# Handing tiles to the output stage earlier in a graph message-passing kernel on one Trainium2 core

## The reference

```python
src = node_feature[edge_src]
parts = [relu(node_feature)]
for t in range(3):
    msg = where(edge_type == t, relu(src @ W_e[t].T + b_e[t]), 0)
    parts.append(segment_sum(msg, edge_dst, num_segments=N))
agg = concatenate(parts, axis=1)                       # 6250 x 512
updated[n] = (agg @ W_n[node_type[n]].T + b_n[node_type[n]])[n]
out = layernorm(x + updated + x)
```

## Time and profile before

| | us |
|---|---|
| median of 3 runs | 906.05 (905.99 to 906.22) |
| the profiled execution | 907.5 |
| its span, first to last instruction | 905.7 |
| mean granted PE clock | 0.912 of full speed |

### The profile page before, as it was taken

One profiled execution on the slowest core, in us unless ns is written; L12 is line 12 of the kernel. 1 busy time (PEld: TensorE's weight loads), 2 busy tenths in 40 slices (PEclk: granted clock), 3 DMA queues, 4 the chain that ended last, 5 costly groups with the idle time before them and its releaser, 6 DMA issues.

```text
span 905.7 us, 14050 instructions
## 1 busy us (share of the span) xinstructions
PE 716.2 (79%) x4555; PEld 598.9 (66%) x4555; DVE 616.4 (68%) x1468; ACT 145.0 (16%) x397; POOL 673.7 (74%) x719
## 2 busy tenths in 40 slices
PE   5593056887997988888898878989888798769786
PEld 3362056776876876676687766878767587658674
DVE  7999988476676557557575754775675477656656
ACT  3393000111111101111110120110112011001120
POOL 7777777777777777777777777777777777777772
PEclk9796569998999989999999998999899999989989
DMA  8595533433443343343344342434435334324321
GB/s 245 161 311 147 136 97 76 113 97 50 146 117 105 97 110 107 103 111 92 94 118 116 96 115 78 121 107 111 106 96 114 93 85 118 102 63 128 97 53 45
DMA packets 72065, 101.39 MB, mean 112 GB/s; under 512 B 18137, under 2 KB 55517, under 8 KB 71995
## 3 DMA queue, kind: packets, MB, share of 16 engines
q0 software_dynamic: 22432, 45.99, 21.3%
q1 hardware_dynamic: 46861, 50.45, 18.5%
q10 hardware_dynamic: 2702, 4.08, 1.5%
HBM read 87.47 MB, written 12.97 MB: 111 GB/s over the span
## 4 chain that ended last, share of the span: by engine, by line
POOL 44%; PE 18%; issue 16%; DVE 15%; DMA 6%; SPq 0%; DVEq 0%; POOLq 0%; ACT 0%; ACTq 0%
POOL tab L753 44%; DMA tab<-message_table,idx_t 5%; PE ps L1652 5%; PE ps L1755 3%; PE ps L1673 3%; DVE src_wide L1098 1%; DVE stage L1131 1%; PE ps L1690 1%; PE ps L1686 1%; DVE first_wide L1034 1%; PE ps L1748 1%; DMA dst_raw<-in_dst 1%; PE ps L1631 1%; DVE dst_raw L1091 1%; PE ps L1698 1%
## 5 line engine op out<-in xcount | busy, mean ns | idle before, releaser
L753 POOL DMA_INDIRECT tab<-message_table,idx_t x630 | 595.2, 945 | 194.1 <-issue 185.6
L1652 PE MATMUL ps<-work,tab 128*128 128x126 f32 x1260 | 180.4, 286 | 94.0 <-DMA tab<-message_table,idx_t 68.7
L1252 DVE TENSOR_TENSOR work<-key_t,ps 128x378 f32<-128x378 f32 (+1 forms) x180 | 108.8, 606 | 208.3 <-PE ps L1652 203.7
L1652 PEld LDWEIGHTS ps<-work,tab 128*128 128x128 f32 x1260 | 163.6, 199 | 106.2 <-issue 68.4
L1264 DVE TENSOR_TENSOR acc<-ps,acc 128x126 f32 (+1 forms) x306 | 96.2, 314 | 30.0 <-DVE acc L1264 9.9
L1755 PE MATMUL ps<-wn_t,stage 128*128 128x384 f32 x282 | 104.8, 512 | 0.0
L749 POOL DMA_INDIRECT xg<-in_x,esrc_t x67 | 72.4, 1081 | 20.7 <-issue 16.8
L1755 PEld LDWEIGHTS ps<-wn_t,stage 128*128 128x128 f32 x282 | 56.3, 200 | 40.4 <-issue 5.6
L1673 PE MATMUL ps<-first_wide,tab 128*128 128x128 f32 x450 | 62.8, 291 | 9.5 <-DVE first_wide L1328 6.5
L1673 PEld LDWEIGHTS ps<-first_wide,tab 128*128 128x128 f32 x450 | 58.9, 207 | 9.9 <-issue 9.9
L896 ACT ACTIVATE stage<-ps 128x128 f32<-128x128 f32 x47 | 12.9, 277 | 297.0 <-PE ps L1755 282.1
(11 more groups left out here) (260 smaller groups left out, 1021.4 us busy)
## 6 DMA issues: line engine op xcount, KB each, us to landing
tab<-message_table,idx_t POOLq DMA_INDIRECT x630, 2.6
message_table<-tab SPq DMA_DIRECT2D x24, 384.0 KB, 3.5
dst_raw<-dense_types SPq DMA_DIRECT2D x45, 192.0 KB
wn_raw<-message_table SPq DMA_DIRECT2D x22, 384.0 KB, 3.4
src_wide<-dense_lists SPq DMA_DIRECT2D x45, 128.0 KB, 3.2
we_raw<-early_types SPq DMA_DIRECT2D x18, 192.0 KB
be_b<-early_types SPq DMA_DIRECT2D x18, 192.0 KB
work<-in_x ACTq DMA_DIRECT2D x10, 256.0 KB, 5.0
```

The costliest lines, as they stand in the source:

```text
L753: pool.indirect_dma_start(msg[:, slot, :], None, table, bass.IndirectOffsetOnAxis(ap=rows, axis=0)).then_inc(signal, 16)
L1252: dve.tensor_tensor(hot[:, first:first + n, :].rearrange("p c (t w) -> p c t w", w=WIN), keys.broadcast_to((P, n, T, WIN)), iota_win.rearr ...
L1652: ins = pe.matmul(sums_bank(j, g), msg[:, column, :], hot[:, column, :], start=(c == 0), stop=(c == n - 1))
```

## The change

- `TAKEN_LATE` goes from 3 to 2: 42 tiles are finished in the quarters, and only tiles 42, 43 and 44 in the last iteration.
- `tile_turns` gives each tile its first quarter. Up to tile 32 it is 4(t+3) as before. From tile 33 on it is the latest of 4(t+2), the dense round's quarter `turn_at(t+1)` + 3, and three quarters after the tile before: 143, 146, 150, 153, 156 for tiles 33 to 37, then 160, 164, 168, 172 for 38 to 41. Before, tiles 33 to 37 had 144, 148, 152, 156, 160, and tile 41 came in the last iteration.
- The last extra tile's linear product moves from quarter 154 to 156.
- In PE's quarter `finish_linear` now stands ahead of `place_selfs`. ACT masks a tile's self messages two quarters ahead of its turn.
- In the last iteration PE does both remaining linear products ahead of the last group's sum, and only the three type products of tile 44 after it. Tile 43's accumulator is read once groups 0 and 1 of the last iteration are added. For that the check gets a bound: the last row must not start below node 5632 (`affine_select` on `limit`, with a wait for the iota ahead of it).
- SP stores in another order at the end; `finish_h` gets a wait for the DVE's own `finish_y` of the tile before.

```diff
-TAKEN_LATE, LATE = 3, 4
+TAKEN_LATE, LATE = 2, 4
+def tile_turns():
+    at = []
+    for t in range(SPLIT):
+        if t < LEAD_FROM - LATE + 1:
+            at.append(NG * (t + LATE - 1))
+        else:
+            at.append(max(NG * (t + LATE - 2), turn_at(t + 1) + ADD_LATER - ACC_LATER, at[-1] + NG - 1))
+    return at
...
-LINEAR_AT = [next(q for q in range(at + 2, at + 6) if q % NG == 2) for at in EXTRA_AT]
+LINEAR_AT = [next(q for q in range(at + 2, at + 8)
+                  if (q % NG == 2 or q >= NG * LEAD_FROM) and tile_step(q, LINEAR_LATER) is None
+                  and tile_step(q - 1, LINEAR_LATER) is None) for at in EXTRA_AT]
...
             pool.iota(limit[:, :], pattern=[[P // 2, 2]], base=-P, channel_multiplier=P // 2,
-                      allow_small_or_imprecise_dtypes=True)
+                      allow_small_or_imprecise_dtypes=True).then_inc(limit_made, 1)
+            pool.wait_ge(limit_made, 1)
+            pool.affine_select(out=limit[:, :], in_=limit[:, :], compare_op=ALU.not_equal, fill=float(NA * P),
+                               base=-(HR - 1), pattern=[[0, 2]], channel_multiplier=1)
...
                 add_sums(j, 0, bases_of[0])
                 add_sums(j, 1, bases_of[1])
-                finish_acc(SPLIT + 1, Z0_TILES - 1, 0, ADDED["main", j, 1])
+                finish_acc(NA - 1, 0, 3, ADDED["main", j, 1])
+                finish_h(SPLIT - 1, SPLIT - 1)
                 finish_h(SPLIT, 0, 2)
+                finish_y(SPLIT - 1, SPLIT - 1)
+                dve.wait_ge(group_summed, NG * j + 3)
                 add_sums(j, 2, bases_of[2])
-                finish_y(SPLIT - 1, SPLIT - 1)
                 finish_y(SPLIT, 0, 2)
+                finish_h(NA - 1, 0, 3)
                 dve.wait_ge(group_summed, NG * j + 4)
                 add_sums(j, 3, bases_of[3])
                 finish_acc(ORDER[KE], KE, 1, ALL_ADDS)
-                finish_acc(NA - 1, 0, 3, ALL_ADDS)
-                finish_h(SPLIT + 1, Z0_TILES - 1)
+                finish_y(NA - 1, 0, 3)
                 finish_h(ORDER[KE], KE, 1, slot=SLOT_OF[KE])
-                finish_y(SPLIT + 1, Z0_TILES - 1)
-                finish_h(NA - 1, 0, 3)
                 finish_y(ORDER[KE], KE, 1, slot=SLOT_OF[KE])
-                finish_y(NA - 1, 0, 3)
...
-                t = tile_step(q, 1)
-                if t is not None:
-                    place_selfs(t, t)
                 t = tile_step(q, LINEAR_LATER)
                 if t is not None:
                     extras = sum(at < q for at in LINEAR_AT)
                     finish_linear(t, first=t == 0, behind=extras if extras else None)
+                t = tile_step(q, 1)
+                if t is not None:
+                    place_selfs(t, t)
...
                 sum_group(j, 1)
-                finish_linear(0, 2, first=True)
-                pe.wait_ge(stage_acc[2], 1)
-                finish_turn(SPLIT + 1, Z0_TILES - 1, len(BATCHES))
                 pe.wait_ge(added, ADDED["dense", j, SIDES - 1])
                 finish_turn(NA - 1, 0, len(BATCHES), 3, first=True)
                 pe.wait_ge(fin_var[1], KE)
                 finish_turn(ORDER[KE], KE, NZ, 1)
+                place_selfs(NA - 1, 0, 3)
+                place_selfs(ORDER[KE], KE, 1)
+                finish_linear(0, 2, first=True)
                 pe.wait_ge(added, ADDED["main", j - 1, NG - 1])
                 sum_group(j, 2)
-                place_selfs(SPLIT + 1, Z0_TILES - 1)
-                place_selfs(NA - 1, 0, 3)
-                place_selfs(ORDER[KE], KE, 1)
+                finish_linear(0, 3, first=True)
                 pe.wait_ge(hot_ready, NG * NI)
                 pe.wait_ge(d_hot, NI)
+                linear_open(KE, 1)
                 pe.wait_ge(added, ADDED["main", j, 1])
-                linear_open(KE, 1)
                 sum_group(j, 3)
-                finish_linear(Z0_TILES - 1)
                 linear_types(KE, 1)
-                finish_linear(0, 3, first=True)
```

More of the change, by code:

```diff
@@ L119 @@
 BATCHES = ([(0, 1)] + [(1 + QUAD * m, QUAD) for m in range(QUADS)] + [(1 + QUAD * QUADS, NA - 1 - QUAD * QUADS)])
-TAKEN_LATE, LATE = 3, 4
+TAKEN_LATE, LATE = 2, 4
 SPLIT = NA - TAKEN_LATE
-Z0_TILES = SPLIT + 1
-STORES = len(BATCHES) - 1 + TAKEN_LATE
+Z0_TILES = SPLIT
+STORES = len(BATCHES) - 1 + BATCHES[-1][1]
 SETS_OF_TILES = 4
-assert sum(n for _, n in BATCHES) == NA and BATCHES[-1] == (SPLIT, TAKEN_LATE)
+assert sum(n for _, n in BATCHES) == NA and BATCHES[-1] == (SPLIT - 1, TAKEN_LATE + 1)
 XB = 4
@@ L171, with tile_step @@
 ACC_LATER, LINEAR_LATER, H_LATER, SD_LATER, Y_LATER = 2, 4, 5, 6, 7
+def tile_turns():
[6 more added lines that the diff above has]
+    return at
+TILE_AT = tile_turns()
+TILES = {at: t for t, at in enumerate(TILE_AT)}
+assert TILE_AT[-1] == NG * (NI - 2)
+def tile_step(q, later):
+    return TILES.get(q - later)
 LIMIT_STEP = 15
@@ L194 @@
 assert PAIR_OF[-1] == NE - 1 and SLOT_OF[KE] + 1 + T <= ET
-def tile_step(q, later):
-    t = (q - later) // NG - (LATE - 1)
-    return t if (q - later) % NG == 0 and 0 <= t < SPLIT else None
 def count_adds():
@@ L394, in build @@
         iota_moved = sem("iota_moved")
+        limit_made = sem("limit_made")
         hot_iota_set, acc_zeroed, limits_set = sem("hot_iota_set"), sem("acc_zeroed"), sem("limits_set")
@@ L669, in _ @@
                     store_fin(tile, tiles)
+            sp.wait_ge(fin_y[0], Z0_TILES)
+            store_fin(SPLIT - 1)
+            sp.wait_ge(ctl_set, 1)
+            need = sp.value_load(ctl[0:1, 0:1], min_val=0, max_val=1)
             sp.wait_ge(fin_y[2], 1)
             store_fin(SPLIT)
[L672 to L676, removed]
             sp.wait_ge(fin_y[3], 1)
             store_fin(NA - 1)
+            store_extra(KE)
             sp.wait_ge(stored[0], 16 * STORES)
@@ L932, in quarter @@
                     dense_relu(dense_step(q, MAKE_LATER))
-                if g == 2 and j > 1:
-                    mask_selfs(j - 2)
+                if tile_step(q, -2) is not None:
+                    mask_selfs(tile_step(q, -2))
+                if q == NG * (NI - 1) - 2:
+                    mask_selfs(SPLIT)
                 if q + 2 in EXTRAS:
@@ L941, in last_iteration @@
                 finish_x(0, 2, first=True)
-                mask_selfs(SPLIT + 1)
-                mask_selfs(SPLIT + 2)
+                mask_selfs(NA - 1)
                 mask_selfs(ORDER[KE])
-                finish_x(Z0_TILES - 1)
                 finish_x(0, 3, first=True)
@@ L949, in last_iteration @@
                 finish_sd(0, 2)
-                finish_sd(Z0_TILES - 1)
                 finish_sd(0, 3)
@@ L1366, in finish_h @@
                 dve.wait_ge(fin_xt[z], nth + 1)
+                if isinstance(nth, int) and nth > 0:
+                    dve.wait_ge(fin_y[z], nth)
                 fin_link(dve.tensor_tensor(h[z][:, :], x_tile, x_tile, ALU.add), nth, z, 1)
@@ L1437, in quarter @@
                     self_masks()
-                if tile_step(q, ACC_LATER) is not None:
-                    finish_acc(tile_step(q, ACC_LATER), tile_step(q, ACC_LATER), 0, ADDED["main", j - 1, NG - 1])
+                t = tile_step(q, ACC_LATER)
+                if t is not None:
+                    finish_acc(t, t, 0, max(ADDED["main", t + 1, NG - 1], ADDED["dense", t + 1, SIDES - 1]))
                 if q - 1 in EXTRAS:
@@ L1459, in last_iteration @@
                 dve.wait_ge(group_summed, NG * j + 2)
-                finish_h(SPLIT - 1, SPLIT - 1)
-                dve.wait_ge(group_summed, NG * j + 3)
                 add_sums(j, 0, bases_of[0])
                 add_sums(j, 1, bases_of[1])
-                finish_acc(SPLIT + 1, Z0_TILES - 1, 0, ADDED["main", j, 1])
+                finish_acc(NA - 1, 0, 3, ADDED["main", j, 1])
+                finish_h(SPLIT - 1, SPLIT - 1)
                 finish_h(SPLIT, 0, 2)
+                finish_y(SPLIT - 1, SPLIT - 1)
+                dve.wait_ge(group_summed, NG * j + 3)
                 add_sums(j, 2, bases_of[2])
-                finish_y(SPLIT - 1, SPLIT - 1)
                 finish_y(SPLIT, 0, 2)
+                finish_h(NA - 1, 0, 3)
                 dve.wait_ge(group_summed, NG * j + 4)
@@ L1785, in quarter @@
                     finish_linear(t, first=t == 0, behind=extras if extras else None)
+                t = tile_step(q, 1)
+                if t is not None:
+                    place_selfs(t, t)
                 if q in EXTRA_LINEAR:
                     n = EXTRA_LINEAR[q]
-                    done = sum(tile_step(before, LINEAR_LATER) is not None for before in range(q))
+                    done = sum(tile_step(before, LINEAR_LATER) is not None for before in range(q + 1))
                     finish_linear(n, 1, first=n == 0, behind=done)
```

## The result

The changed kernel takes 927.6 us (median of 4 runs, 926.4 to 928.1) against 906.1 for the kernel before on the same chip: ratio 1.0234, 95% interval 1.0216 to 1.0252, so it is 2.3% slower. The prediction had the sign and the places, but 918.6 us and a range that ended at 924.0.

The account below looks back on a forecast made before the run. POOL's gather issue rate was taken as the bound, with PE and VectorE out of slack near quarter 157. From 906.05 us, POOL losing 16.1 and the end saving 3.5 gave 918.6 us; 8-in-10 range 908.5 to 924.0.

Parts of the forecast that it names:

- What bounds, and the mechanism: Gathers: POOL's issue rate bounds until PE, waiting in turns with VectorE, is late; POOL loses 16.1 us.
- Four turn waits and one product wait: PE at turns of tiles 34 to 37 and tile 36's product: waits of 3.8, 4.5, 3.0, 3.9 and 5.6 us.
- The clock term: PE behind each of five waits: half clock costs 1.65 us; without any, POOL loses 8.5 us; that rival had 0.08.
- The page beside it: Skill page on PE's half rate after waits: 0.83 us lost per wait, making the sum some 4 us lower.
- The walk: PE and VectorE queues stepped from quarter 144: gather (41,1) begins at 840.6 instead of 824.55.
- The product of tile 36 in quarter 157: PE must wait there for VectorE's `finish_h` of the extra tile in the same quarter, 5.6 us.
- The end: Last landing to last store: six matmuls after the last sum instead of more; 3.5 us saved, bounds 2.5 and 4.7.
- The start: Before the first gathers: the select and iota wait are hidden, 0 us, bounds 0 and +0.2.
- POOL's waits: Gathers (38,3), (40,1) and (40,2): waits for PE's sums grow from at most 1.1 us to 4 to 8 us.
- ScalarE's copy ahead of `place_selfs`: PE at tiles 33, 34, 36 and 37: waits about 0.5 us each for the copy, bounds 0.4 and 0.8.
- Span and median: Whole kernel: span 918.3 us, profiled execution 920.1; median 1.45 us below that execution, 918.6 us.
- the bank is shared: PE's turns: a tile's turn waits for `finish_acc` of the tile before, since both use one PSUM bank.

Follow-up runs that it names:

- keep_warm: Changed kernel plus idle filler matmuls ahead of the turns of tiles 34 to 37 and tile 36's linear product; 916.5 us, ratio 1.0116 to the kernel before.
- lin_bank6: Changed kernel with the last extra tile's linear product in free PSUM bank 6, so it and tile 36's don't wait for each other; 919.3 us, ratio 1.0142.
- turns_only: Changed kernel with the old last iteration put back (tiles 41 to 44 in it), new quarters for tiles 33 to 40 kept; 931.4 us, ratio 1.0266.
- end_only: Kernel before with its old quarters, plus the check's bound and the new last-iteration order for four tiles; 907.1 us, ratio 1.0005.
- spread: Changed kernel with the four quarters of lead given in single steps over tiles 20 to 41, three extra products moved; 969.3 us, ratio 1.0693.
- end_lin6: Kernel before with old quarters, the new four-tile end and bound, and the last extra tile's product in its own bank; ratio 0.9982, 904.4 us on 906.05.
- turn_bank36: Changed kernel with even tiles from 36 on transposed into a second PSUM bank, so their turn skips the wait for the previous tile; 926.2 us, ratio 1.0225.

## Why the prediction was off

- **What bounds, and the mechanism: right.** POOL keeps its 1.25 us beat until PE's sums come late; they come late through waits in turns between PE and VectorE. Four turn waits and one product wait, of the forecast length within 0.6 us each, at the forecast places.
- **The clock term: this step failed.** The prediction took 1.65 us for the half clock behind each of the five waits. Compared row by row with the same shapes at full rate, the kernel after loses about 3.6 us behind turn 34 (from 753 to 761), 1.7 behind turn 35, 3.0 behind turn 36, 2.7 behind turn 37 and 1.5 behind the product: 12.5 against 8.25. `keep_warm` takes off 9.9 us in the trace and 10.7 by the ratios, where the sum had 7.6; it can't give back all 12.5, since its filler ahead of turn 35 runs at half rate itself (20 rows in 3.59 us) and holds PE some 0.8 us longer than the wait did. The 1.65 was read from the kernel before, and there it was nearly right. The rows at half rate behind its three waits, each with the next row:

```profile
784.65 2.21 PE L1673 MATMUL ps<-dense_f,tab 128*128 128x128 f32 x10
786.70 0.83 PE L1652 MATMUL ps<-work,tab 128*128 128x126 f32 x6
...
796.65 3.79 PE L1755 MATMUL ps<-wn_t,stage 128*128 128x384 f32 x6
800.27 0.83 PE L1686 MATMUL ps<-we_t,order_f 128*128 128x128 f32 x6
...
814.76 1.65 PE L1690 MATMUL ps<-we_t,order_f 128*128 128x128 f32 x6
816.21 1.81 PE L1673 MATMUL ps<-first_wide,tab 128*128 128x128 f32 x10
817.86 1.28 PE L1673 MATMUL ps<-dense_f,tab 128*128 128x128 f32 x10
```

  Summed whole, these stretches cost 1.7 us (behind the wait of 2.96), 1.7 (behind 3.17) and 2.1 (behind 4.96). So the wrong thing was to carry a price from old waits over to new ones: even at these rows' mean of 1.8 the five would have cost 9.2. Why the new stretches are longer stays open. It isn't the length of the wait: 4.19 us was followed by a loss of 3.6, 4.52 by 1.7.
- **The page beside it.** The Trainium skill, TensorE: Matmul & The Clock Gate, section HAM oscillation, has 1.67 us at half rate per wait in its example, so a loss of 0.83 us. The prediction put its weight on the trace's own 1.65 instead, and the measured 1.5 to 3.6 are about two to four times the page's.
- **The walk otherwise: 1.7 us short.** (41,1) began 5.9 us later than walked (846.49 against 840.6), and 4.2 of them are the clock's (12.5 - 8.25). The walk also started late: the turn of tile 34 passed at 753.3, not 754.0, so the other steps are 2.4 us too short. One us of that is VectorE's quarters 151 and 152, 8.5 us where 7.5 was taken; the rest is spread over the later steps.
- **The product of tile 36 in quarter 157: right in kind**, 5.6 forecast and 5.78 measured. `lin_bank6` prices the pair at 8.3 us.
- **The end: right**, 3.5 forecast, 3.6 in the trace, 2.9 by `turns_only`. As a result of its own, though, it was taken as if it could be had alone; `end_only`, with tile 41 still in the last iteration, gained 1.1 us in its trace and nothing that its runs could tell.
- **The start: right that it is hidden.** The select takes 0.18 us, the first gather goes out at 3.43 instead of 3.22, and the fifth, at 8.58, no longer waits for ScalarE. The 0.9 us by which iteration 36 is late is no price of the select that the traces can tell: in the profiled executions of the kernels with the select, `spread` left out, that gather begins anywhere from 731.25 (`end_only`) to 733.03 (`end_lin6`).
- **POOL's waits: right in the main.** Forecast were 4 to 8 us at (38,3), (40,1) and (40,2); they were 3.48, 6.70 and 7.90, with three smaller ones.
- **ScalarE's copy ahead of `place_selfs`: right**, 0.52 us each, four times.
- **Span and median.** The sum's own target, the span, was 918.3 and is 924.5, 6.2 us off: 5.8 in POOL's loss (21.9 against 16.1), the rest behind the last store. Nearly all of the other 2.8 us, of the 9.0 between 918.6 and 927.6, is spread between runs: the profiled execution of before was 1.45 us above its median, that of after 1.2 us below its own. That should have widened the range.
- **Where the reason was too simple.** The prediction said that the turn waits *because* the bank is shared. `turn_bank36` shows, for turns 36 and 37, that VectorE's late quarter holds up whichever PE step comes next.

## What to carry to other kernels

In a pipeline staged by hand over two in-order engines, moving a step is not free because its slack looks large: look at what the other engine does in the quarter where the step lands, and ask of each wait what comes next if it is gone. Price a long wait of TensorE with the whole slow stretch behind it, summed over all rows until shapes take their usual time again, and give that price a wide range: the stretches of the kernel before (1.7 to 2.1 us) didn't tell those of the kernel after (1.5 to 3.6). Where a wait can't be removed, filler matmuls inside it can give back the clock, but only where nothing ready stands behind them.

## What was unexpected of the hardware

- The granted clock could be bought back inside the waits: 0.86 to 0.98 in the window from 732 to 840 with 62 idle-time matmuls of 128x128, and 10.7 us of 927.6 by the ratios.
- The slow stretch behind a wait of 3.5 to 5.8 us was not of one length: between 1.5 and 3.6 us were lost, and the longest wait (5.78 us) cost the least. No run here shows what sets the length.
